# GpSimd issues a slot's result chunks and row lists in turn, one of each

## What is computed

```python
z1 = jnp.einsum('bfi,bir->bfr', x, v[:, 0]) / inch
z = jnp.einsum('bfr,bor->bfo', z1, u[:, 0]) / r
y = jnp.einsum('bfi,oi->bfo', x, W) + fc_bias + z + b
return jax.nn.gelu(y, approximate=False)
...
prob = jax.nn.softmax(xf @ w_router + b_router, axis=-1)
_, idx = jax.lax.top_k(prob, TOP_K)
mask = (idx[:, :, None] == jnp.arange(N_BLOCKS)[None, None, :]).any(axis=1)
h = jax.nn.relu(jnp.einsum('nd,ebd->neb', xf, w1b) + b1b[None])
y = jnp.einsum('neb,ebd,ne->nd', h, w2b, mask)
y = y + b2[None, :]
...
x = x + _L0_ffn_ref(_L0_cond_ref(...), ...)
```

## Time and profile before

| what | value |
|---|---|
| median of the runs | 1310.8 us (1292.05, 1310.8, 1319.59) |
| span of the profiled execution | 1288.1 us |
| PE busy | 911.6 us, 71% |
| DVE busy | 828.0 us, 64% |
| ACT busy | 584.8 us, 45% |
| POOL busy | 584.3 us, 45%, 589 instructions |
| mean DMA rate | 275 GB/s |

### The profile page before, as it was taken

One profiled execution on the slowest core, in us unless ns is written; L12 is line 12 of the kernel. 1 busy time (PEld: TensorE's weight loads), 2 busy tenths in 40 slices (PEclk: granted clock), 3 DMA queues, 4 the chain that ended last, 5 costly groups with the idle time before them and its releaser, 6 DMA issues.

```text
span 1288.1 us, 17916 instructions
## 1 busy us (share of the span) xinstructions
PE 911.6 (71%) x4924; PEld 702.2 (55%) x4924; DVE 828.0 (64%) x1964; ACT 584.8 (45%) x1061; POOL 584.3 (45%) x589
## 2 busy tenths in 40 slices
PE   8887789889899998888898774898898981000000
PEld 7664567677677766666676553677676761000000
DVE  4444355666556665556656563877687867987777
ACT  5434345565556555465546453765566560000000
POOL 1455664555565655555565655454455543000000
PEclk9988789989999999999999896999999996555555
DMA  5777577776787777777876765787888759999999
GB/s 173 266 241 272 190 245 278 263 258 228 252 272 264 252 263 256 246 259 242 269 261 235 254 237 220 239 261 236 288 271 259 232 166 357 414 429 429 426 430 385
DMA packets 103234, 354.82 MB, mean 275 GB/s; under 512 B 29961, under 2 KB 29961, under 8 KB 92384
## 3 DMA queue, kind: packets, MB, share of 16 engines
q1 hardware_dynamic: 59104, 217.21, 49.6%
q0 software_dynamic: 43936, 136.37, 27.0%
q10 hardware_dynamic: 96, 0.10, 0.0%
HBM read 200.47 MB, written 169.65 MB: 287 GB/s over the span
## 4 chain that ended last, share of the span: by engine, by line
PE 46%; another core or an unknown queue 13%; DMA 12%; DVE 11%; issue 8%; ACT 7%; ACTq 2%; DVEq 1%; POOL 0%; POOLq 0%; SPq 0%
PE yps L1201 10%; DMA w2l<-yt 10%; PE lay L1068 9%; PE trn L1158 8%; PE hid L1173 7%; PE hid L1178 4%; DVE gsb L744 3%; PE hid L1054 3%; PE trn L1088 2%; DVE stx L935 2%; ACT gsb L578 2%; DMA outT<-ys 2%; ACTq L589 1%; PE rps L1103 1%
## 5 line engine op out<-in xcount | busy, mean ns | idle before, releaser
L744 DVE TENSOR_TENSOR gsb<-trn,gsb 128x512 fp32r<-128x512 f32 x286 | 192.0, 687 | 258.3 <-ACT gsb L578 216.5
L498 POOL DMA_INDIRECT yt<-ys,ids x218 | 235.2, 1079 | 244.9 <-ACT ys L637 177.3
L472 POOL DMA_INDIRECT xg<-grow,ix x224 | 221.4, 988 | 139.6 <-DVE ix L818 74.2
L1158 PE MATMUL trn<-idf,gr 128*128 128x128 f32 x1144 | 185.6, 287 | 106.4 <-DVE gsb L744 101.1
L1158 PEld LDWEIGHTS trn<-idf,gr 128*128 128x128 f32 x1144 | 140.3, 146 | 170.1 <-DVE gsb L744 135.8
L1068 PE MATMUL lay<-w2l,xs 128*128 128x512 f32 x768 | 201.7, 414 | 0.0
L578 ACT ACTIVATE gsb<-trn 128x512 fp32r<-128x512 f32 x286 | 171.6, 600 | 30.1 <-PE trn L1158 16.5
L1068 PEld LDWEIGHTS lay<-w2l,xs 128*128 128x128 f32 x768 | 151.4, 201 | 33.1
L606 ACT ACTIVATE hv<-hid,b1c 128x512 f32<-128x512 f32 (+1 forms) x94 | 52.6, 584 | 222.6 <-PE hid L1178 106.8
L1201 PE MATMUL yps<-w2c,hh 128*128 128x512 f32 x368 | 140.6, 465 | 6.2 <-issue 4.5
L1173 PE MATMUL hid<-gsb,w1c 128*128 128x512 f32 (+1 forms) x576 | 133.2, 374 | 8.0 <-issue 7.8
(11 more groups left out here) (184 smaller groups left out, 1518.4 us busy)
## 6 DMA issues: line engine op xcount, KB each, us to landing
gr<-xg SPq DMA_DIRECT2D x49, 1056.0 KB
xs<-yt SPq DMA_DIRECT2D x16, 2048.0 KB, 19.5
w2l<-yt SPq DMA_DIRECT2D x15, 2048.0 KB, 19.7
gr<-xg SPq DMA_DIRECT2D x45, 528.0 KB
stx<-xT SPq DMA_DIRECT2D x64, 256.0 KB, 4.2
outT<-ys SPq DMA_DIRECT2D x31, 512.0 KB, 20.4
xg<-xrow SPq DMA_DIRECT2D x16, 528.0 KB
w2f<-xrow SPq DMA_DIRECT2D x16, 512.0 KB
```

The costliest lines, as they stand in the source:

```text
L472: pool.indirect_dma_start(out=xg, out_offset=bass.IndirectOffsetOnAxis(ap=ix[:, row_buffer(b), q, k:k + 1], axis=0), in_=grows[row_buffer( ...
L498: pool.indirect_dma_start(out=yt, out_offset=bass.IndirectOffsetOnAxis(ap=ids[:, j % 8, c:c + 1], axis=0), in_=yss[result_buffer(j)][:, c, ...
L744: dve.tensor_tensor(gsb[:, :, LO, c * P:(c + 1) * P], trn[n % 2][:, :].rearrange("p (k t) -> p k t", k=KC), gsb[:, :, HI, c * P:(c + 1) * ...
L1158: last = pe.transpose(trn[n % 2][:, k * P:(k + 1) * P], gr[:, j % 2, c, k * P:(k + 1) * P], idf[:, :])
```

## The change

`place_rows` is split in two. Its waits become `rows_chosen(b)`, which stands ahead of everything else in every slot that has row lists. Its four DMAs become four calls of `place_row(b, q, k)`. In slots 31 to 66 a loop over c then issues chunk c of the tile and row list c in turn. Slots up to 30 and from 67 on keep their order: rows first, then chunks.

```diff
--- before.py
+++ after.py
@@ -462,16 +462,17 @@
                 pool.affine_select(out=sumk[:, :], in_=sumk[:, :], compare_op=ALU.not_equal, fill=1.0, base=-2 * NE * k,
                                    pattern=[[-1, NE]], channel_multiplier=1).then_inc(g_s, 1)
 
-            def place_rows(b, q):
+            def rows_chosen(b):
                 pool.wait_ge(v_ix, b + 1)
                 j = 4 * (b - RING + 3) - 1
                 if j >= 0:
                     pool.wait_ge(s_gr[j % 2], 32 * (j // 2 + 1))
                     pool.wait_ge(s_gr[1 - j % 2], 32 * ((j - 1) // 2 + 1))
-                for k in range(TOPK):
-                    pool.indirect_dma_start(
-                        out=xg, out_offset=bass.IndirectOffsetOnAxis(ap=ix[:, row_buffer(b), q, k:k + 1], axis=0),
-                        in_=grows[row_buffer(b)][:, q, :], in_offset=None).then_inc(s_sc[row_buffer(b)][q], 16)
+
+            def place_row(b, q, k):
+                pool.indirect_dma_start(
+                    out=xg, out_offset=bass.IndirectOffsetOnAxis(ap=ix[:, row_buffer(b), q, k:k + 1], axis=0),
+                    in_=grows[row_buffer(b)][:, q, :], in_offset=None).then_inc(s_sc[row_buffer(b)][q], 16)
 
             def place_tiles(n):
                 pool.wait_ge(v_tb, n + 1)
@@ -504,13 +505,16 @@
                 b, q = divmod(s, 4)
                 j = s - LAG - 2
                 first = s <= LAG + 2 or SLOTS + 3 <= s
-                if 0 <= s - 7 < SLOTS and first:
-                    place_rows((s - 7) // 4, (s - 7) % 4)
-                if 0 <= j < NTILE:
-                    for c in range(chunks(j)):
+                if 0 <= s - 7 < SLOTS:
+                    rows_chosen((s - 7) // 4)
+                    for k in range(TOPK):
+                        if first:
+                            place_row((s - 7) // 4, (s - 7) % 4, k)
+                for c in range(TOPK):
+                    if 0 <= j < NTILE and c < chunks(j):
                         send(j, c)
-                if 0 <= s - 7 < SLOTS and not first:
-                    place_rows((s - 7) // 4, (s - 7) % 4)
+                    if 0 <= s - 7 < SLOTS and not first:
+                        place_row((s - 7) // 4, (s - 7) % 4, c)
                 if q == 0 and 2 <= b <= NB:
                     place_tiles(b - 2)
                 if s == 4 * (NB + 1) + 1:
```

## The result

The changed kernel takes 1351.4 us (median; 1348.3 to 1359.2), the kernel before 1309.5 us beside it. The ratio is 1.0375, with an interval of 1.026 to 1.049. I had forecast no change. It is slower by 42 us.

What follows compares the result with a forecast made beforehand. TensorE, busy for 71% of the span, was read as first, with GpSimd following. Terms 0, 0 to 1 and 0 on the profiled 1288.1 us gave 1288 to 1289, or 1311 on the runs' median scale; range 1290 to 1330.

Steps and rivals of the forecast that it cites:

- GpSimd is late for nobody: Slots 31 to 62: GpSimd follows the others, has 4.4 us to spare per slot and delays nobody the chain knows.
- Rival B: ScalarE's unnamed waits for hidden values come from four row lists in one run; spreading gains up to 35 us; chance 0.08.
- Part 1: Three slots of four, without a wait for `ix`: last row list 1.0 us earlier, last chunk 2.8 us later; 0 us.
- Part 2: First slot of each batch, wait for `ix` ahead of chunks: last row list 5 us later; 0 to 1 us.
- it has caught up by then: Slot after slot 59: GpSimd's eight DMAs and table list end at 665.5, caught up with 0.3 us.
- my longest landing: Row lists' landing, bounded by SyncE's tile loads at 3.7 to 6.0 us; the longest is 6.0 us.
- The cover of 5.15 us: Step 36: ScalarE idles 5.15 us before the hidden values, so a late GELU costs 0 us on the path.
- The 0 to 14 us for late GELUs: Eight first slots whose row lists a GELU needs: 8 x 1.7 = 14 us at most without cover, taken as 0 to 1.
- rival C: Slot 63 or a catch-up fails by one or two us in a few batches: 9 to 18 us slower; chance 0.12.
- rival A: Late row lists reach the path through landings longer than read: 17 to 33 us slower, 1328 to 1344; chance 0.14.
- Part 3: Last slots, 63 to 66, where GpSimd is behind: 1.1 us to spare at worst, 0.7 us gained on one load; 0.
- 0.12 for slower: Whole kernel: chance 0.12 of measuring slower, against 0.06 faster and 0.82 same, with about 2% (26 us) as the threshold.

Runs made afterwards that it cites:

- all_short_2: Kernel before plus a pause of three memsets behind every four DMAs of slots 7 to 70, where the kernel before takes 1312.4 us: 1204.0 us, ratio 0.923.
- alt_3of4: Changed kernel, but the first slot of each batch keeps the old order and old wait; against the kernel before (1318.5 us): 1318.8 us, ratio 1.001.
- after_third: Changed kernel, unaltered, run where the kernel before takes 1123.1 us: 1133.1 us, ratio 1.0074.
- all_one_2: Kernel before plus a one-memset pause behind every four DMAs of slots 7 to 70, second run, kernel before at 1123.1 us: 1125.2 us, ratio 1.002.
- alt_paused: Changed kernel plus a seven-memset pause behind each fourth DMA of slots 31 to 66; against the kernel before (1318.5 us): 1293.5 us, ratio 0.982.
- after_split: Changed kernel plus one seven-memset pause behind each batch's first slot; against the kernel before (1122.8 us): 1134.4 us, ratio 1.009; again 1137.4 us, 1.012.
- before_short: Kernel before plus a two-memset pause between chunks and row lists of slots 31 to 66; against the kernel before (1312.4 us): 1282.2 us, ratio 0.984.
- before_paused: Kernel before plus a seven-memset pause between chunks and row lists of slots 31 to 66; against the kernel before (1318.5 us): 1304.6 us, ratio 0.990.
- all_one: Kernel before plus a one-memset pause behind every four DMAs of slots 7 to 70, kernel before at 1122.8 us: 1126.1 us, ratio 1.003.
- all_short: Kernel before plus a three-memset pause behind every four DMAs of slots 7 to 70, where the kernel before takes 1122.8 us: 1163.9 us, ratio 1.037.

## Why the prediction was wrong

**"GpSimd is late for nobody": the step that failed.** The busy times, the chain without GpSimd and the waits were read rightly, and so was the slot (14.6 us, 10.2 of them work; by the page's means of 1,079 and 988 ns for a chunk and a row list it is 10.7). The conclusion wasn't right. I took an engine's effect on the others to be its products: landed lists and landed chunks. In the held condition it also acts by how it issues, and for that the profile has no name but "unknown". What the runs showed in its place: the early wait joins two slots' DMAs to runs of 16, TensorE's results are held until 1.4 to 2.3 us behind them, and a batch takes 62.7 us instead of 58.3. That path stood at 0 us in my sum.

**Rival B was the right place with the wrong sign and the wrong unit.** It tied the unnamed waits to runs of four row lists, and the run of four at 643.90 was evidence against. That evidence was sound: runs of four with a gap of a microsecond ahead are mostly clean (71 of 80 in all_short_2), and the one at 643.90 has 1.03 us ahead of it. But in the other slots the row lists follow the chunks without a gap, so the runs are of seven and eight. For slot 60 the group gives the first chunk and the table list at 661.72 that ended the run. I split the run by what its DMAs carry. Nor did I ask what the change does to it: alternating two kinds keeps the run, where I had priced B as a spreading.

**Part 1 was right in the time.** alt_3of4: 1.001. That it nevertheless adds 59 us of unnamed waits, none of them on the path as far as the time shows, the part did not have.

**Part 2 had the events and missed what they make.** The working had the catch-up (first slot done at 654.1, eight more DMAs to 665.5, "it has caught up by then"). That is the unbroken run of 16. I priced it by whether its products came in time. In the changed kernel the last list of slot 35 is issued by 323.77, and the GELU that needs it starts at 336.42, 12.6 us later, twice my longest landing, and its releaser is unnamed. The cover of 5.15 us that I gave step 36 was such a wait itself: I counted as slack what was already the cost that grew. The moved wait brings 4.4 us a batch. What of that would be left without held increments isn't measured in this condition; in the free one the changed stretch is 6 us longer over eight batches.

**In the free condition the number fits, and by luck in part.** The 0 to 14 us for late GELUs met 8 to 10 us there (1133.1 against 1123.1; 1.0074), which is rival C's size. ScalarE's wait for row lists in after_third:

```profile
ACT grow L565 <- DMA xg<-grow,ix: 76.0, 25, 7.1
```

And all_one_2:

```profile
ACT grow L575 <- DMA xg<-grow,ix: 18.9, 10, 3.0
```

So rival A's mechanism is real, covered for the greater part as I said (57 us more of waiting, 6 of time). Its landing can be read now, since 27 of the 32 GELUs of steps 32 to 63 are released by row lists in after_third. The last row list of slot 35 there:

```profile
256.83 0.97 POOL L473 DMA_INDIRECT xg<-grow,ix  x1 [0.30 <-issue]
```

The GELU of step 36, which it releases:

```profile
260.41 0.60 ACT L565 ACTIVATE grow<-lay 128x512 f32<-128x512 f32 x1 [2.36 <-DMA xg<-grow,ix]
```

It had landed 3.6 us after its start, near the lower of my bounds (3.7). The last one of slot 59, and the GELU of step 60:

```profile
547.39 0.97 POOL L473 DMA_INDIRECT xg<-grow,ix  x1 [0.30 <-issue]
```

```profile
555.45 0.60 ACT L565 ACTIVATE grow<-lay 128x512 f32<-128x512 f32 x1 [7.09 <-DMA xg<-grow,ix]
```

That is 8.1 us, beyond the larger bound (6.0) and beyond the 6.9 us from which I had rival A cost time in step 60. The 27 lie between 3.4 and 8.1 us. So my landing was too short by up to 2 us, and the sum came out near the measured time without having it right. The Trainium skill (DMA: Bandwidth & Descriptors, Anatomy of one DMA — SWDGE (gpsimd) path) gave an estimate of 2.6 us; every one of the 27 is longer, beside other traffic of some 300 GB/s.

**Part 3** can't be judged closely: slots 63 to 66 lie in another surrounding, and the 18 us stall behind slot 70 is gone from the changed trace. Up to the end of the span the two traces differ by 7 us more than at step 63.

**The chances.** 0.12 for slower was too low, and the range ended at 1330. 13% of the chain had a releaser without a name. I knew of 104.6 us of it, gave it one rival, priced from one pattern, and only on the side of a gain. A cost of unknown cause in the stretch that a change touches should have widened both sides.

**What stays open.** That runs without a gap, the condition and the early wait together make the held loss is shown: with the pauses the loss is gone though the early wait is there (alt_paused), and in the free condition it is 0.7%. That the runs of 16 alone carry it is argued from the traces; the kernel that parts only these runs (after_split) met the free condition twice. The length of a run isn't the whole rule: between 100 and 750 us a bunch stands behind 27 of 32 runs of 7 to 9 before, 16 of 19 after, and 9 of 10 longer ones after, but behind only 1 of 8 runs of 7 to 9 in before_short, and 8 of 10 runs of four in alt_3of4. These eight stand 0.70 to 0.72 us behind three chunks, so a gap of 0.7 us doesn't seem to part a run. But in before_paused six of the eight runs of four with 1.7 to 1.8 us ahead of them have a bunch too; a gap of that length isn't a sure cure either. What puts a chip into one condition or the other isn't known. One rival is untested: each time on record comes with a span and a clock from the profile, and in the held condition the profile's own events are missing while GpSimd writes descriptors. So nothing here tells whether the recording takes part in the delay. Not known either is the path by which GpSimd's issue holds TensorE's increments, or whether a gap of 0.4 us (all_one) would help: it is the safest in the free condition (1.002 to 1.003) and never ran in the held one. No kernel is shown to beat the one before in both conditions; all_short is 8% faster in the one and 4% slower in the other.

## What to carry to other kernels

- A wait whose releaser has no name, in the stretch that a change touches, is a term of the sum. Look what another engine did without a break just before each, whatever its instructions carry, and ask what the change does to that pattern, in both directions.
- A wait moved ahead of ready work makes a burst later. Price the burst, not only the lateness of its products.
- Before a verdict on a small scheduling change, see that it holds in a second series: the same edit was 3.75% in one condition and 0.7% in the other, and a cure for the one was a cost in the other.
- A landing read in one place is one draw. The same transfer took 3.4 to 8.1 us in one execution.

## What the runs showed of the hardware

- In one condition of the chip, TensorE's semaphore increments reach other engines late while GpSimd issues indirect DMAs with only 0.30 us between them. They appear together 0.7 to 2.3 us behind the run's end (336.4 behind 334.64; 677.23 behind 675.81). Of the runs of 7 to 9 before, 27 of 32 have it, of those of four with a gap of 1.2 us around them (all_short_2) 9 of 80; in the traces of the free condition no run has it. The longest wait was 18.23 us, behind 29 DMAs. Gaps of 1.2 us behind every four DMAs halve the unnamed waits (229 to 110 us) and take 108 us off the time (1312.4 to 1204.0). Increments of VectorE and ScalarE took effect in such a run (0.04 us at 329.83), though many have no event in the trace.
- In the other condition runs of 33 to 85 DMAs hold nothing up (after_third, no unnamed wait), and the kernel before takes 1123 us instead of 1310. The same chip showed both.
- An indirect scatter of 264 KB landed 3.4 to 8.1 us after its start in after_third.
- The granted clock was lower where TensorE stood: over the stretch it was 0.92 with TensorE busy for 84% of it (422.70 of 502) and 1.00 where it was busy for 99% (388.89 of 392).
